# Products for the maxima of the last head group, laced into the subtraction of an attention kernel

## The reference

```python
x = x + xattn(layernorm(x), ctx, Wq, bq, Wk, bk, Wv, bv, Wo, bo)
x = x + ffn(layernorm(x), router_w, router_b, weights1, bias1, weights2, bias2)

# xattn, for each batch b and head h
scores = (q @ k.T) / sqrt(16)
attn = softmax(scores, axis=-1)
ctx = attn @ v                      # heads joined, then @ Wo.T + bo

# ffn
e = argmax(x @ router_w.T + router_b)
y = relu(relu(x @ weights1[e] + bias1[e]) @ weights2[e] + bias2[e])
```

## Time and profile before

| | us |
|---|---|
| median of 3 runs (lowest to highest) | 1159.52 (1156.99 to 1161.11) |
| profiled execution | 1164.71 |
| its span | 1162.9 |
| PE busy | 1069.2 |
| VectorE busy | 908.3 |
| GpSimd busy | 847.5 |
| ScalarE busy | 830.1 |

### The profile page before, as it was taken

One profiled execution on the slowest core, in us unless ns is written; L12 is line 12 of the kernel. 1 busy time (PEld: TensorE's weight loads), 2 busy tenths in 40 slices (PEclk: granted clock), 3 DMA queues, 4 the chain that ended last, 5 costly groups with the idle time before them and its releaser, 6 DMA issues. The chain is left out here.

```text
span 1162.9 us, 38973 instructions
## 1 busy us (share of the span) xinstructions
PE 1069.2 (92%) x15015; PEld 883.2 (76%) x15015; DVE 908.3 (78%) x2321; ACT 830.1 (71%) x1892; POOL 847.5 (73%) x1613
## 2 busy tenths in 40 slices
PE   5998999999999999999999999999998249999992
PEld 4786888878888888888888888888886249877772
DVE  4887788888888888888888888888888248767672
ACT  4776787878888788878788878888786226656551
POOL 4435677777787777787778777777766747777776
PEclk9999999999999999999999999999999669999997
DMA  7515222532222222232322222222210346676650
GB/s 242 168 56 129 75 76 75 122 102 76 75 76 75 80 84 79 84 88 80 94 81 79 75 76 75 75 76 76 71 53 21 110 142 205 208 210 203 204 155 12
DMA packets 91155, 120.38 MB, mean 104 GB/s; under 512 B 14096, under 2 KB 73883, under 8 KB 90781
## 3 DMA queue, kind: packets, MB, share of 16 engines
q1 hardware_dynamic: 77150, 84.04, 25.7%
q0 software_dynamic: 13824, 33.85, 8.1%
HBM read 60.61 MB, written 59.31 MB: 103 GB/s over the span
## 5 line engine op out<-in xcount | busy, mean ns | idle before, releaser
L466 ACT ACTIVATE arena<-sc 128x512 f32<-128x512 f32 x512 | 264.5, 604 | 92.9 <-PE sc L806 76.2
L583 DVE TENSOR_REDUCE mx<-maxima 128x4 bf16<-128x512 f32 (+1 forms) x384 | 311.9, 838 | 5.0 <-PE maxima L784 5.0
L417 POOL DMA_INDIRECT out<-arena x160 | 157.1, 982 | 59.8 <-issue 32.9
L383 POOL DMA_INDIRECT pages<-row,slot_i x128 | 130.6, 1020 | 56.7 <-issue 54.6
L797 PE MATMUL sc<-qk 32*128 32x256 f32 x2048 | 151.4, 393 | 0.3 <-DVE xnT L603 0.3
L822 PE MATMUL sc<-wo_s,aT 128*128 128x256 f32 x512 | 133.1, 383 | 5.2 <-ACT arena L466 3.0
L815 PE MATMUL pA<-arena 128*32 128x128 f32 x4096 | 137.6, 275 | 0.0
L543 ACT ACTIVATE arena<-sc 128x256 f32<-128x256 f32 x160 | 61.3, 383 | 84.7 <-PE sc L992 83.4
L608 DVE STREAM_TRANSPOSE tr<-pA 128x512 f32<-128x512 f32 x128 | 90.6, 708 | 38.6 <-PE pA L815 38.4
L815 PEld LDWEIGHTS pA<-arena 128*32 128x32 f32 x4096 | 106.5, 110 | 10.6 <-issue 4.8
L784 PE MATMUL maxima<-qk 32*128 32x128 bf16 x2048 | 103.5, 217 | 9.8 <-issue 4.1
(11 more groups left out here) (138 smaller groups left out, 2612.3 us busy)
## 6 DMA issues: line engine op xcount, KB each, us to landing
arena<-pages SPq DMA_DIRECT2D x160, 130.0 KB, 2.6
cT<-ctxT SPq DMA_DIRECT2D x64, 256.0 KB, 4.2
xs<-x_in SPq DMA_DIRECT2D x128, 128.0 KB, 3.5
pages<-empty SPq DMA_DIRECT2D x120, 130.0 KB, 3.5
pages<-empty SPq DMA_DIRECT2D x1, 5200.0 KB, 19.8
out<-arena POOLq DMA_INDIRECT x160
w2s<-w SPq DMA_DIRECT2D x1, 2080.0 KB
qk<-w SPq DMA_DIRECT2D x1, 2064.0 KB, 8.1
```

Of the source, the lines that this page charges most:

```text
L383: pool.indirect_dma_start(pages, bass.IndirectOffsetOnAxis(slot_i[:, u:u + 1], 0), row[:, q % 4, u, :], None, bounds_check=last_slot, oob_ ...
L417: pool.indirect_dma_start(out_rows, bass.IndirectOffsetOnAxis(pr[:, r, COL_TOKEN:COL_TOKEN + 1].bitcast(U32), 0), pr[:, r, 0:D], None, bou ...
L466: act.activation(pt[:, u % 2, g].rearrange("p i k -> p (i k)"), sc[g][:, :], ACT.Exp).then_inc(S["exp_out"], 1)
L583: dve.tensor_reduce(mx[:, :].rearrange("p (g h) -> p g h", h=32)[:, g:g + n, 0:4], mball[:, 512 * b:512 * (b + n)].rearrange("p (g h k) -> ...
```

## The change

The products of group 3 go to pA instead of `mb[0]`. They stand no longer behind the subtraction but inside it: one of the four behind each step of the second pair, and the first of them waits for the transpose that empties pA. So that group 3 isn't in the second pair, the order of the groups is 0, 3, 1, 2, for the subtraction and for the exponentials. The projection goes to `mb[0]` and waits for the first maximum; the products of the next chunk wait for the copies out of `mb[0]`; the attention, which writes pA, waits for the last maximum. Waits for exponentials that name a place in their order move by one or two places.

```diff
         def proj_bank(q, n):
-            return (pA, mb[2], mb[0], mb[1])[n] if q == 0 else pA
+            return (pA, mb[2], mb[0], mb[1])[n] if q == 0 else mb[0]
+        EXP_ORDER = (0, 3, 1, 2)
...
             def exps(q, u):
-                for g in range(4):
-                    after(act, "T_done", 16, q, 4 * u + g)
+                for k, g in enumerate(EXP_ORDER):
+                    after(act, "T_done", 16, q, 4 * u + k)
...
             def maxima(q, u, g, n):
-                b = g % 3
+                src = pA[:, :] if g == 3 else mball[:, 512 * g:512 * (g + n)]
...
+            def score_for_max(q, u, g, j):
+                m, c = j // 2, j % 2
+                rows = slice(32 * g, 32 * g + 32)
+                return pe.matmul((mb[0], mb[1], mb[2], pA)[g][:, j * P:(j + 1) * P], qMh[rows, q % 2, m, c, u * P:(u + 1) * P],
+                                 kTh[rows, q % 2, c, u * P:(u + 1) * P], start=True, stop=True)
...
-            def subtract_max(q, u):
+            def subtract_max(q, u, qn, un):
                 after(pe, "mxT_out", 4, q, u)
-                for pair in ((0, 1), (2, 3)):
+                for pair in (EXP_ORDER[0:2], EXP_ORDER[2:4]):
                     for j in range(4):
                         for g in pair:
...
+                        if pair == EXP_ORDER[2:4] and live(qn):
+                            q1, u1 = back(q, u, 1)
+                            if j == 0 and live(q1):
+                                after(pe, "tr_out", 4, q1, u1)
+                            last_group_for_max(qn, un, j)
...
                         if live(s):
                             after(pe, "mxT_out", 4, s, u)
-                        scores_for_max(qn, un, (0, 1, 2))
+                            lq, ln = chunk_of(*back(s, u, 1))
+                            if live(lq):
+                                after(pe, "proj_out", 4, lq, ln)
+                        scores_for_max(qn, un)
...
-                        subtract_max(s, u)
-                    if live(qn):
-                        after(pe, "max_out", 16, qn, 4 * un)
-                        scores_for_max(qn, un, (3,))
+                        subtract_max(s, u, qn, un)
+                    elif live(qn):
+                        for j in range(4):
+                            last_group_for_max(qn, un, j)
                     if live(pq):
-                        if live(q1):
-                            after(pe, "tr_out", 4, q1, u1)
-                        elif pq == 1 and n == 1:
-                            after(pe, "proj_out", 4, 1, 0)
+                        if live(qn):
+                            after(pe, "max_out", 16, qn, 4 * un)
...
                     if live(q1):
-                        after(pe, "exp_out", 16, min(s, NQ - 1), 4 * u + 1 if live(s) else 13)
+                        after(pe, "exp_out", 16, min(s, NQ - 1), 4 * u + 2 if live(s) else 14)
                         project_out(q1, u1)
...
                         if live(s):
-                            after(pe, "exp_out", 16, s, 4 * u + 2)
+                            after(pe, "exp_out", 16, s, 4 * u + 3)
...
                         after(pe, "exp_out", 16, s, 4 * u + 3)
-                        if live(pq):
-                            after(pe, "proj_out", 4, pq, n)
+                        if live(qn):
+                            after(pe, "max_out", 16, qn, 4 * un + 3)
                         else:
                             after(pe, "tr_out", 4, q1, u1)
                         attend(s, u)
```

More of the change, by code:

```diff
@@ L581, in maxima @@
                 after(dve, "S_done", 8, q, 2 * u + g // 3)
-                b = g % 3
+                src = pA[:, :] if g == 3 else mball[:, 512 * g:512 * (g + n)]
                 dve.tensor_reduce(mx[:, :].rearrange("p (g h) -> p g h", h=32)[:, g:g + n, 0:4],
-                                  mball[:, 512 * b:512 * (b + n)].rearrange("p (g h k) -> p g h k", g=n, h=4), AX.X,
+                                  src.rearrange("p (g h k) -> p g h k", g=n, h=4), AX.X,
                                   ALU.max).then_inc(S["max_out"], n)
@@ L777, in values, with scores_for_max, last_group_for_max @@
                 ins.then_inc(S["V_done"], 1)
-            def scores_for_max(q, u, groups):
-                for j in range(4):
[L781 to L785, removed]
+            def score_for_max(q, u, g, j):
[3 more added lines that the diff above has]
+                                 kTh[rows, q % 2, c, u * P:(u + 1) * P], start=True, stop=True)
+            def scores_for_max(q, u):
+                for j in range(4):
+                    for g in range(3):
+                        ins = score_for_max(q, u, g, j)
                 ins.then_inc(S["S_done"], 1)
+            def last_group_for_max(q, u, j):
+                ins = score_for_max(q, u, 3, j)
+                if j == 3:
+                    ins.then_inc(S["S_done"], 1)
             def max_transpose(q, u):
```

## The result

| | before, us | after, us |
|---|---|---|
| median (lowest to highest), 4 runs each | 1160.32 (1156.99 to 1163.00) | 1142.76 (1142.13 to 1145.18) |
| profiled execution, its span | 1164.71, 1162.9 | 1142.81, 1141.0 |
| PE busy | 1069.2 | 1048.5 |
| VectorE, GpSimd, ScalarE busy | 908.3, 847.5, 830.1 | 911.2, 847.5, 824.8 |

The changed kernel takes 0.9847 of the time before, with a 95% interval of 0.9829 to 0.9864: 17.6 us less between the medians. The forecast was 1138, the range 1127 to 1151: the time lies inside it, 4.8 us above the forecast.

What follows compares the result with a forecast made beforehand. A ring through TensorE and VectorE was taken to bound the loop. Chunk gains 0.13 + 0.19 + 0.14 + 0.25 = 0.71 us a turn, times 123 / 4, gave 21.8, taken as 21.5, off the median 1159.5: 1138, range 1127 to 1151.

Steps and rivals of the forecast that it cites:

- p from PE's own order: p is the start of a chunk's projection; TensorE's own queue was to set it at a + 0.52 us.
- a + 0.52: Predicted projection start, where a is the start of the chunk's first subtraction; ends a + 0.49 and a + 0.60.
- The spacing: Time between successive matmuls of one row group on TensorE, taken as 0.06 us, seven of them making 0.42.
- The term of u = 0: Predicted gain in chunk u = 0: 0.24 us, less 0.05 lost waiting for the third maximum, so 0.19.
- VectorE's limit: Earliest projection start VectorE allows: m + 0.06, put at a + 0.33 (u = 1, 3) or a + 0.44 (u = 0, 2).
- m: The end of VectorE's first maximum in a chunk.
- the ring: Main-loop cycle: attention products, VectorE's transpose, first maximum (0.65 us), four products (0.33 us), projection, rest of chunk to attention.
- The waits: Added or moved waits on transpose, copies, third maximum and exponentials, each behind cover; in the loop they were to cost zero.
- VectorE's limit everywhere: Rival: projection at m + 0.06 in every chunk, 1.16 us a turn, 35.7 us gained, about 1124; chance 0.08.
- Little left: Rival: switch to projection or mid-stream wait costs 0.1 us more, gain 11 us, 1148.5; chance 0.20 for gains 0 to 12.
- the slower queue: Rival: group 3's eight matmuls spaced 0.152 us as loads don't overlap; 57 us lost, 1216; turns at 0.087; chance 0.06.
- Lockstep by pairs: Rival: the sixteen subtractions run pair by pair, eight rounds with the products; a + 0.52 again, so nothing changes.

Runs made afterwards that it cites:

- the run with the order alone: The kernel before with only the group order 0, 3, 1, 2 for subtraction and exponentials; products and banks stay: 1162.92 us, ratio 1.0017.
- doubling: The changed kernel with each of the four products of group 3 issued twice: 1161.24 us, ratio 0.9997 to the kernel before.
- the moved statistics: The changed kernel with the fourth batch's row statistics moved from chunk u = 3 to u = 2: 1188.14 us, ratio 1.0225 to the kernel before.

## Why the prediction was right, and where not

**p from PE's own order.** Predicted a + 0.52, measured 0.54 from a start that is itself 0.04 earlier (the lead of group 3, seen alone in the run with the order alone), so 0.50 on the old scale. The spacing is 0.057 us as measured by doubling, not 0.06; seven of them make the difference. The 0.144 us from the last product to the projection is unchanged: 399.17 + 0.33 - 0.214 = 399.286, then 399.43. The weight load did not add to the spacing, as the earlier trace rows had said. The rule of the Trainium skill (TensorE: Matmul & The Clock Gate, Part 3, The mechanism), that a weight load overlaps running matmuls only for another row group, had said otherwise; 0.057 us is less than the load's own 0.092.

**Gains by chunk.** From the earlier trace rows and the rows above, the periods of u = 3, 0, 1, 2 were 6.98, 6.77, 6.54, 6.91 and are 6.83, 6.76, 6.38, 6.64: gains of 0.15, 0.01, 0.16, 0.27 against 0.13, 0.19, 0.14, 0.25 predicted. Three terms were right to 0.02. The term of u = 0 was wrong.

**The step that failed.** "VectorE's limit, p = m + 0.06 at the earliest: ... a + 0.44 for u = 0" kept m where it stood against a before, as if VectorE moved with p. Measured, m is 0.58 us after a in u = 0 instead of 0.37, and only 0.04 of that is the earlier a. The reason is a chain that leaves PE before the subtraction of u = 3 and comes back to it at the first maximum of u = 0. In u = 2, where VectorE is late too, m did move with p: it is at a + 0.42, the 0.39 of before and the 0.04. Timeline of all engines, first of the kernel before, 410 to 420 us, then of the kernel after, 396 to 406 us; L839 and L854 are the matmuls that rank the tokens, L303 and L305 GpSimd's addition.

```profile
410.74 0.26 PE L839 MATMUL sc<-hot,ones_b 128*128 128x96 bf16 x3
...
411.59 0.25 POOL L334 TENSOR_TENSOR need<-rks,room 128x32 f32<-128x32 f32 x1 [1.87 <-ACT rks L498]
...
416.43 2.40 POOL L303 TENSOR_TENSOR xs<-xs,bo_s 128x1024 f32<-128x1024 f32 x1
418.00 0.90 DVE L642 TENSOR_TENSOR_SCAN run<-fresh,run,zer 128x32 f32<-128x32 f32 x1
```

```profile
396.41 0.26 PE L854 MATMUL sc<-hot,ones_b 128*128 128x96 bf16 x3
...
397.26 0.25 POOL L336 TENSOR_TENSOR need<-rks,room 128x32 f32<-128x32 f32 x1 [1.47 <-ACT rks L500]
...
402.10 2.40 POOL L305 TENSOR_TENSOR xs<-xs,bo_s 128x1024 f32<-128x1024 f32 x1
```

From the ranking matmuls at the end of u = 2 to the addition it is 5.69 us in both kernels (410.74 to 416.43, 396.41 to 402.10): ScalarE copies the ranks, and from 411.59 and 397.26 on GpSimd's instructions fill it one after another; the addition takes 2.40, the scan ends 0.07 or 0.08 us behind it, and the statistics, the transpose and the first maximum follow without a gap. From the ranking to m of u = 0 it is 420.61 - 410.74 = 9.87 before and 406.29 - 396.41 = 9.88 after. This stretch runs through u = 3 into u = 0 and cannot shrink by what PE saves. What can shrink is m to p, from 0.39 to 0.06. And of these 0.33 the late third maximum takes 0.15: the transpose of the maxima starts at 409.30, behind the maximum that ends at 409.25, 2.95 us after p where 2.80 would do. The 0.18 that is left is what u = 3 and u = 0 gain together (0.16 by the periods). The prediction had seen the last loss, at 0.05, and not the chain before it. That the scan, caught beside the addition, is the link is shown by moving it: u = 0 then gains 0.21 us a turn, and the ratio falls from 0.9847 to 0.9785, some 7 us of 1160.

**The sum.** 123/4 x 0.59 = 18.1 us where 21.8 stood; 17.6 were measured between medians. Of the 4.8 us between forecast and result this makes 3.4 (the prediction took 21.5); 0.8 is the median of the kernel before, 1160.3 with its fourth run and not 1159.5; the rest lies within the interval. Setting the sum against the median and not the profiled execution was right: from the first subtraction to the last that execution took 868.9 us, and the run with the order alone, of the same turn, 863.0, so some 6 us of it were stalls outside the ring. The kernel after took 846.2. Prologue and tail were taken as nothing, and between the two profiles they cancel in part. The first subtraction comes 2.0 us earlier (31.16 to 29.14), but so it does with the order alone (29.11). From the last subtraction to the last scatter of tokens it is 39.4 us before and 41.6 after, with all other kernels here between; whether the change has a part in that is not shown.

**The waits.** Zero, as costed: PE shows no wait for the transpose out of pA or for the copies, and 0.2 us in all for exponentials. That the transpose is in time is not safe, as the moved statistics showed.

**The rivals.** VectorE's limit everywhere did not come: in three chunks p is 0.12 to 0.23 us behind m. It came in one chunk, and by a cause that the rival did not name. Little left and the slower queue fall with the spacing of 0.057, well under the 0.087 at which the queue turns. Lockstep by pairs, the last rival, did not come either: all sixteen subtractions still start within 0.25 us (398.88 to 399.12). What the prediction did not foresee is that the lacing itself is worth nothing, since the products overtake.

## What to carry to other kernels

When a step is taken out of a ring, follow for each chunk of the pattern the chain that ends last back past the ring, to the event where it leaves it, and check whether the saved time lies inside or outside that stretch. A short instruction of VectorE whose duration differs from place to place (the scan took 0.30 us in one kernel and 1.07 in another) can hide a wait that no idle row shows: look at what GpSimd runs beside it, and move one of the two. A bank that is free at the right moment was worth four fifths of this change and the order of the groups the rest; lacing the products between the subtractions was worth nothing.

## What the runs showed of the hardware

- Matmuls of different row groups do not keep the order of the program in their starts: the products in one block behind the subtractions start at 400.41, ahead of two subtractions at 400.42; and in the earlier trace rows a score matmul starts at 426.00, ahead of products at 426.04 that stand before it. The Trainium skill (TensorE: Matmul & The Clock Gate, Part 3, The mechanism) says that matmuls keep program order in start and end; the starts here do not.
- Whether the ends do is only suggested. With long score matmuls ahead of the last products in the program, VectorE was released 0.34 us late although the products had started in time; with the same scores behind them it was not. Matmul ends are modelled in these rows, so this was not shown more directly.
- The scan took 0.30 us where it started ahead of GpSimd's addition, and 0.90, 1.07, 1.18 and 2.21 us where it started beside it, ending 0.07 or 0.08 us behind it each time; the normalisation took 0.42 us and, beside a subtraction on GpSimd, 2.58, ending 0.29 behind that. The Trainium skill (SBUF — State Buffer, Who interferes with whom) says that a VectorE instruction with two inputs in SBUF contends with a GpSimd instruction that reads SBUF, through a port pair that is an exclusive lock. The trace agrees: here VectorE's instruction ended only once GpSimd's had.
